# Attention, FFN and mixture of experts on one core: row maxima by way of DRAM, three-pass up products, one table set at the start

## The reference, cut to what matters

```python
x = x + xattn0(layernorm(x), ctx)        # 16 heads of 8, softmax over 256 keys
x = x + ffn0(layernorm(x))               # butterfly up, gelu, butterfly down, 512 hidden
x = x + xattn1(layernorm(x), ctx)        # 16 heads of 8
x = x + moe(layernorm(x))                # 16 experts of 64, top 4, and a shared one

scores = einsum('bhqd,bhkd->bhqk', q, k) / sqrt(8)
attn   = softmax(scores, axis=-1)
out    = einsum('bhqk,bhkd->bhqd', attn, v)
...
h = gelu(butterfly(x @ W_exp + b_exp, up_weights) + up_bias)
```

## Time and profile before

| what | us |
|---|---|
| median of 3 runs | 209.72 (208.79 to 210.5) |
| the profiled execution | 209.94 |
| its span in the trace | 207.8 |

### The profile page before, as it was taken

How to read it: one execution, slowest core, us unless ns; L and a number is a source line. 1 busy time by engine, 2 the same in 40 slices (tenths; PEclk the granted TensorE clock), 3 DMA queues, 4 the chain that set the end, 5 groups by cost and what they waited for, 6 DMA issues and landing times.

```text
span 207.8 us, 4287 instructions
## 1 busy us (share of the span) xinstructions
PE 197.7 (95%) x1727; PEld 110.7 (53%) x1727; DVE 154.2 (74%) x243; ACT 146.7 (71%) x262; POOL 55.6 (27%) x72
## 2 busy tenths in 40 slices
PE   7798899999999999997999999999999999999993
PEld 4464367564574543443344566554566745766640
DVE  0399989899998764259975989999775664795482
ACT  2865873989886999972795998987999936613230
POOL 7948940039046000059000000040000252300400
PEclk9999999999999999999999999999999999999999
DMA  6950000000004400000000000000000352003641
GB/s 177 323 224 3 0 0 5 2 3 0 3 0 131 197 3 0 0 5 0 0 0 3 0 5 0 3 0 3 0 5 6 122 205 80 0 6 136 179 142 50
DMA packets 5795, 10.50 MB, mean 51 GB/s; under 512 B 1120, under 2 KB 2576, under 8 KB 5648
## 3 DMA queue, kind: packets, MB, share of 16 engines
q1 hardware_dynamic: 4208, 6.16, 9.3%
q0 software_dynamic: 848, 3.53, 4.5%
q10 hardware_dynamic: 720, 0.53, 0.9%
HBM read 9.64 MB, written 0.59 MB: 49 GB/s over the span
## 4 chain that ended last, share of the span: by engine, by line
PE 81%; DVE 7%; ACT 4%; DMA 2%; issue 2%; SPq 1%; POOL 1%
PE PS L363 60%; PE OB L363 21%; DVE T L1003 3%; DMA spread<-comb_out 2%; SPq L658 1%; DVE attn L1033 1%; DMA comb_out<-comb_t 1%; DVE k_lo L940 1%; DVE xn L991 1%; ACT K L830 1%; POOL hid_t L777 1%; ACT sq L853 1%; ACT sq L856 1%; ACT sq L840 0%; DVE x L1047 0%
## 5 line engine op out<-in xcount | busy, mean ns | idle before, releaser
L1003 DVE TENSOR_REDUCE T<-PS 128x4 f32<-128x1024 f32 x64 | 76.6, 1220 | 4.8 <-PE PS L363 4.2
L864 ACT ACTIVATE P<-PS 128x512 f32<-128x512 f32 x128 | 68.1, 603 | 14.0 <-PE PS L363 13.3
L363 PE MATMUL OB<-P,V 128*32 128x256 f32 x512 | 33.4, 384 | 0.1
L363 PE MATMUL PS<-K,Q 32*128 32x256 f32 x256 | 28.2, 323 | 0.5 <-ACT sq L856 0.3
L363 PEld LDWEIGHTS PS<-K,Q 32*128 32x128 f32 x256 | 17.6, 183 | 17.0 <-ACT P L864 6.9
L363 PE MATMUL PS<-Q,K 32*128 32x256 f32 x256 | 25.6, 320 | 0.3
L363 PEld LDWEIGHTS PS<-Q,K 32*128 32x128 f32 x256 | 16.4, 183 | 11.5 <-ACT P L864 5.1
L777 POOL TENSOR_TENSOR hid_t<-spread,prod_t 128x512 f32<-128x512 f32 x7 | 9.3, 1325 | 46.6 <-DMA spread<-comb_out 37.3
L917 ACT ACTIVATE gate_t<-PS 128x512 f32<-128x512 f32 (+1 forms) x18 | 10.3, 596 | 16.1 <-DVE prod_t L1112 12.0
L363 PEld LDWEIGHTS OB<-P,V 128*32 128x32 f32 x512 | 14.3, 109 | 10.6 <-ACT P L864 0.9
L765 POOL TENSOR_TENSOR attn<-o_raw,sums 128x512 f32<-128x512 f32 x4 | 5.1, 1282 | 44.9 <-ACT sums L883 44.8
(11 more groups left out here) (125 smaller groups left out, 324.8 us busy)
## 6 DMA issues: line engine op xcount, KB each, us to landing
spread<-comb_out SPq DMA_DIRECT2D x32, 128.0 KB, 3.0
w_gu<-gu POOLq DMA_DIRECT2D x1, 1024.0 KB, 5.5
w<-w2p POOLq DMA_DIRECT2D x1, 512.0 KB, 5.8
outT<-x SPq DMA_DIRECT2D x2, 256.0 KB, 2.9
e_up<-eup POOLq DMA_DIRECT2D x1, 508.0 KB, 6.1
e_dn<-edn POOLq DMA_DIRECT2D x1, 508.0 KB, 6.4
w_exp<-wexp POOLq DMA_DIRECT2D x1, 258.0 KB, 6.2
x<-xT SPq DMA_DIRECT2D x2, 128.0 KB, 3.0
```

Of the source, the lines that this page charges most:

```text
L363: return nc.tensor.matmul(out, lhsT, rhs, start=start, stop=stop)
L864: finish(nc.scalar.activation(P[:, (JOINT * U + j) % (JOINT * PUNITS), :, :].rearrange("p k q -> p (k q)"), PS[:, FILLED["sc", U, j // 2][ ...
L1003: finish(nc.vector.tensor_reduce(dst, two("max", U, i).rearrange("p j (t s) -> p j t s", t=2), AX.X, ALU.max, negate=True), "red", U, i)
```

## The change

- `turn` and `shift` are gone. `red.U.i` writes into T[:, U, ...] (a place of its own for each unit). A new table for SP holds `st.U` and `ld.U`. `st.U` stores T's 128 x 8 numbers to DRAM so that each of the four heads has a row of 256 there: 1024 single numbers of 4 bytes. `ld.U` waits for that store and reads the four rows of 1 KB into row g, 32 + g, 64 + g and 96 + g of Q. `sc.U` waits for the load's semaphore. RING = 8 semaphores each serve stores and loads.
- `up` multiplies in three passes (high by high, high by low, low by high) in f32r instead of one f32 product. For it `uhi` (ACT) and `ulo` (DVE) split the normed rows, and `fwr.3` writes a high and a low part of the matrix.
- ACT loads the table set for exp and log ahead of its first computation.
- `moeadd` is two additions of half a chunk; SP stores the first half, ACT the second.
- The tables of all engines are written anew: 38 fills for 31, and steps move between engines (`xcopy`: 7 on DVE for 4, `hid`: 9 on POOL for 7).

```diff
 BANKS = 7
-TURNS = 2
 PUNITS = 3
+RING = 8
...
-sc.23.0:16 pv.21 turn.13:2 max.27.0:34 sc.23.1:05 pv.22 max.27.1:12 sc.24.0:06 pv.23 sc.24.1:35 max.28.0:12
...
+sc.23.0:23 qsel.1.1.3:4 pv.21 max.26.0:01 sc.23.1:26 max.26.1:45 pv.22 max.27.0:23 pv.23 sc.24.0:06 sc.24.1:14
...
+SP_ORDER = """
+st.0 ld.0 st.1 st.2 ld.2 ld.1 st.3 st.4 ld.3 st.5 ld.4 st.6 ld.6 ld.5 st.7 ld.7 st.9 st.8 st.10 ld.8 ld.10 ld.9
+st.11 st.12 ld.12 ld.11 st.13 st.14 ld.13 st.15 ld.14 ld.15 st.16 st.17 ld.16 st.19 st.20 st.18 ld.17 ld.18
+ld.19 ld.20 st.21 ld.21 st.22 ld.22 st.23 ld.23 st.24 ld.24 st.25 st.26 ld.25 ld.26 st.27 ld.27 st.28 st.29
+ld.28 ld.29 st.30 st.31 ld.30 ld.31
...
-        T = sb("T", [D, TURNS, 2, D])
+        T = sb("T", [D, UNITS, JOINT, 2], f32r)
...
-        w_up = sb("w_up", [D, BLK, D])
+        w_up_hi, w_up_lo = (sb(n, [D, BLK, D], f32r) for n in ("w_up_hi", "w_up_lo"))
...
+        turn_out = nc.dram_tensor("turn_out", (UNITS, JOINT, 2, D), f32, kind="Internal").ap()
...
-            def turn(t):
-
-                take()
-                for U in reversed(TURN_UNITS[t]):
-                    for i in (1, 0):
-                        after(pe, "red", U, i)
-                if fresh(pe, eye_in, 16):
-                    pe.wait_ge(eye_in, 16)
-                for qt in range(2):
-                    for j in range(JOINT):
-                        rows = slice(32 * j, 32 * j + 32)
-                        last = mm(bank("turn", t)[rows, qt * D:(qt + 1) * D], T[:, t % TURNS, qt, rows], EYE)
-                give(last, "turn", t)
...
-                after(pe, "shift", turned_with(U))
+                turned_waited(pe, U)
...
+            def three(to, w_high, w_low, high, low, start=True, stop=True):
+
+                mm(to, w_high, high, start=start, stop=False)
+                mm(to, w_high, low, start=False, stop=False)
+                return mm(to, w_low, high, start=False, stop=stop)
...
             def up(c, k):
                 take()
-                after(pe, "normed", norm(1, c))
+                after(pe, "ulo", c)
                 after(pe, "fwr", 3)
-                give(mm(bank("up", c, k), w_up[:, k, :], xn[:, chunk(c)]), "up", c, k)
+                give(three(bank("up", c, k), w_up_hi[:, k, :], w_up_lo[:, k, :], n_hi[:, :], n_lo[:, :]), "up", c, k)
...
+            def stored_waited(U):
+                if fresh(sp, turned_out[U % RING], 16 * (U // RING + 1)):
+                    sp.wait_ge(turned_out[U % RING], 16 * (U // RING + 1))
+
+            def store_maxima(U):
+                for i in (1, 0):
+                    after(sp, "red", U, i)
+                if U >= RING:
+                    stored_waited(U - RING)
+                sp.dma_start(turn_out[U].rearrange("j t q -> q j t"), T[:, U, :, :].bitcast(f32),
+                             allow_slow_non_contiguous=True).then_inc(turned_out[U % RING], 16)
+
+            def load_maxima(U):
+                l, b, g = unit(U)
+                stored_waited(U)
+                if U >= RING:
+                    turned_waited(sp, U - RING)
+                sp.dma_start(Q[g:D:32, g, queries(b)].bitcast(f32).rearrange("j (t q) -> j t q", t=2),
+                             turn_out[U]).then_inc(turned_in[U % RING], 16)
+
+            steps = {"st": store_maxima, "ld": load_maxima}
+            for name, *at in SP_STEPS:
+                steps[name](*at)
...
-                after(sp, "moeadd", c)
-                sp.dma_start(outT[:, chunk(c)], x[:, chunk(c)]).then_inc(stored, 16)
+                sp.wait_ge(half_added, c + 1)
+                half = slice(c * CH, c * CH + CH // 2)
+                sp.dma_start(outT[:, half], x[:, half]).then_inc(stored, 16)
             sp.wait_ge(stored, 16 * NCH)
+            sp.wait_ge(stored_too, 16 * NCH)
...
-            nc.gpsimd.memset(T[:, :, :, :].bitcast(u32), 0).then_inc(t_zero, 1)
...
             act.dma_start(w_v[:, :], wv).then_inc(wv_in, 16)
+            tables(EXP_LN)
...
+            def high_rows(c):
+
+                after(act, "normed", norm(1, c))
+                for v in range(NCH):
+                    filled(act, "vproj", v)
+                for p in range(len(SPANS[1])):
+                    filled(act, "kproj", 1, p)
+                if c:
+                    for k in range(BLK):
+                        filled(act, "up", c - 1, k)
+                finish(nc.scalar.activation(n_hi[:, :], xn[:, chunk(c)], ACT.Copy), "uhi", c)
...
+                act.dma_start(outT[:, half], x[:, half]).then_inc(stored_too, 16)
...
-                t = turned_with(U)
                 filled(dve, "max", U, i)
-                if fresh(dve, t_zero, 1):
-                    dve.wait_ge(t_zero, 1)
-                if t >= TURNS:
-                    filled(dve, "turn", t - TURNS)
-                dst = T[:, t % TURNS, :, :].rearrange("p t (j r) -> p j t r", r=32)[:, 2 * i:2 * i + 2, :, g]
-                finish(nc.vector.tensor_reduce(dst, two("max", U, i).rearrange("p j (t s) -> p j t s", t=2), AX.X,
+                finish(nc.vector.tensor_reduce(T[:, U, 2 * i:2 * i + 2, :], two("max", U, i).rearrange("p j (t s) -> p j t s", t=2), AX.X,
                                                ALU.max, negate=True), "red", U, i)
-
-            def shift(t):
-
-                l, b, g = unit(TURN_UNITS[t][0])
-                n = len(TURN_UNITS[t])
-                dst = Q[:, g:g + n, queries(b)]
-                filled(dve, "turn", t)
-                finish(nc.vector.tensor_tensor(dst, bank("turn", t)[:, 0:SEQ].unsqueeze(1).broadcast_to([D, n, SEQ]),
-                                               dst.bitcast(f32), ALU.add), "shift", t)
...
-                finish(nc.vector.tensor_copy(dst, src), "fwr", step)
+                if step == 3:
+                    link(nc.vector.tensor_copy(dst, src))
+                    finish(nc.vector.tensor_tensor(w_up_lo[:, :, :], src, dst.bitcast(f32), ALU.subtract), "fwr", step)
...
+            def low_rows(c):
+                after(dve, "uhi", c)
+                finish(nc.vector.tensor_tensor(n_lo[:, :], xn[:, chunk(c)], n_hi[:, :].bitcast(f32), ALU.subtract),
+                       "ulo", c)
...
-                finish(nc.vector.tensor_tensor(x[:, chunk(c)], OB[:, :], x[:, chunk(c)], ALU.add), "moeadd", c)
+                half = slice(c * CH, c * CH + CH // 2)
+                nc.vector.tensor_tensor(x[:, half], OB[:, 0:CH // 2], x[:, half], ALU.add).then_inc(half_added, 1)
+                half = slice(c * CH + CH // 2, (c + 1) * CH)
+                finish(nc.vector.tensor_tensor(x[:, half], OB[:, CH // 2:CH], x[:, half], ALU.add), "moeadd", c)
```

229 lines of the change are left out of this document (118 added, 111 removed).

## The result

| kernel | median, us | runs | against the kernel before |
|---|---|---|---|
| before, same chip | 209.89 | 4 | |
| changed | 336.88 (335.14 to 339.09) | 4 | 1.608, interval 1.600 to 1.617 |

The change makes the kernel 61% slower, by 127 us. Forecast were 202.9 us and a range of 199 to 210. The mechanism is that of rival 2 (the store lands late and SP becomes the bound), at a size beyond the upper end that I had given it.

What follows compares the result with a forecast made beforehand. PE was taken as the bound, busy 197.7 of 207.8 us, with DVE and ACT close behind in places. Terms -9.2 + 0.5 - 0.3 + 0.5 + 1.2 + 0.5 = -6.8; 209.94 - 6.8 - 0.2 = 202.9 us, range 199 to 210.

Steps and rivals of the forecast that it cites:

- rival 2: SP becomes the bound as stores land late: 215 us for a 6.5 us store, 218.6 for 7.0; chance 0.14.
- The step that failed: Pricing each unit's store of 1024 single numbers from neighbouring packet rows: 2.7 us taken, upper end 7.0.
- Seven rounds of L + 0.5: Layer 1, red.21.1 to red.31.1: SP's seven store-wait-load rounds, L being the store's time; keeps pace up to 4.0 us.
- the 5.4 us of slack: Between max.21.1 and sc.21.0: 12.5 us of other work, less 1.9 for the reduction and 5.2 for the trip.
- The load: Each unit's load of four 1 KB rows behind its store: between 1.6 and 3.0 us, 2.0 taken.
- Turns, up products and fills on PE: On PE, seventeen turns -9.4, three-pass up products -1.8, seven more fills +2.0: -9.2 us in all.
- DVE keeps the steady stretch: In 115 to 150 us DVE keeps its 32.8 us, so the stretch falls by 1.6 only: +1.2 us.
- Rival 1: DVE and ACT are the bound and PE only looks full, so gains there are lost: 206.5 us; chance 0.2.
- Up products -1.8, split +0.5: Three-pass up products save PE 1.8 us; uhi and ulo in the norm, up, gelu chain may show 0.5 at chunk 1.
- Table load 0: At the start, one early table load saves 1.25 us but the new order gives it back: 0, between -1.3 and +1.0.
- Last store -0.3: At the end, storing the first half before the second addition saves 0.3 us, between 0 and 0.6.
- Trips +0.5: Store-and-load trips of 5.2 us are mostly hidden by other work; 0.5 us added for tight places such as start and end.

Runs made afterwards that it cites:

- e7: Changed kernel storing and loading only the maxima of each unit's first 128 queries, 512 single numbers in place of 1024; 341.36 us.
- e13: Changed kernel storing maxima twice: 32 B pieces, which the load reads, and 1024 single numbers 8 B apart; the load waits for both; 299.77 us.
- e9: Changed kernel with maxima stored in 256 pieces of 16 B and read back by four loads per unit, one per head; 264.5 us, ratio 1.254.
- e2: Changed kernel with each store as 128 pieces of 32 B in place of 1024 of 4 B, maxima read back permuted; 207.19 us, ratio 0.987.
- e8b: Changed kernel storing maxima twice: 32 B pieces, which the load reads, and 1024 single numbers 64 B apart; the load waits for both; 233.52 us.
- e8: Changed kernel storing maxima twice: 32 B pieces, which the load reads, and 1024 single numbers 512 B apart; the load waits for both; 217.6 us.
- e5: Changed kernel with only SP's order changed, stores of later units ahead of a unit's load; 379.87 us.
- e1: Changed kernel without its 32 stores and 32 loads; PE waits for the reductions and the maxima are not subtracted; 204.93 us, ratio 0.975.
- e6: The kernel before with only the three-pass up products and their split of tokens and weights; 216.76 us, ratio 1.019.
- e3: Changed kernel storing 32 B pieces by query, with the load reading 1024 single numbers out of DRAM; 243.42 us, ratio 1.158.
- e12: Changed kernel with VectorE turning maxima in 32x32 blocks before the store, one turn and one store for each two units; 222.96 us, ratio 1.047.
- e10: Changed kernel with VectorE turning each unit's maxima in 32x32 blocks, so 128 B pieces go out and back; 210.9 us, ratio 1.000.
- e4: The kernel before, its order kept, with three-pass up products, one table load at the start and halved last store; 212.39 us, ratio 1.010.

## Why the prediction was wrong

**The step that failed** is "64 x 17 ns more gives 2.7 us, 64 x 42 ns gives 4.3, and twice that for a write that also reads 7.0, the upper end". The packets are even cheaper: 0.47 of 16 engines' 1 us, over the 1040 packets of that stretch, is 7 ns each. But a landing is not the sum of packets: the 6.3 us of silence come behind them. What the runs put in its place:

| store of a unit | pieces | separate writes in each 64 B | in each 512 B | landing, us |
|---|---|---|---|---|
| changed kernel | 1024 of 4 B, side by side | 16 | 128 | 10.4 |
| e7 | 512 of 4 B, side by side | 16 | 128 | 9.7 |
| e13 | 1024 of 4 B, 8 B apart | 8 | 64 | 6.6 |
| e9 | 256 of 16 B, side by side | 4 | 32 | 2.7 |
| e2 | 128 of 32 B, side by side | 2 | 16 | 1.4 |
| e8b | 1024 of 4 B, 64 B apart | 1 | 8 | 3.8 |
| e8 | 1024 of 4 B, 512 B apart | 1 | 1 | 3.1 |

What is shown: single numbers land later the closer they lie, at the same count, and half as many at the same closeness land about as late. What is not shown is a law. If the writes within 64 B cost one another, it is 0.44 us for each further one, (10.4 - 3.8) / 15, which gives 6.9 for e13 against 6.6 measured, and nothing for the difference of e8b and e8. If it is those within 512 B, it is 0.057 us for each, (10.4 - 3.1) / 127, which gives 6.7 for e13 and 3.5 for e8b against 6.6 and 3.8. Both estimates fit; both mix the distance with the order of the partitions, and neither holds for larger pieces (e9 and e2 land sooner than e8b). Whether the DMA engine or the memory holds the writes up, no run tells.

The Trainium skill's DMA: Bandwidth & Descriptors, section Specifications, has an engine read, modify and write below 512 B. That rule puts e2's, e8's and the changed kernel's pieces on the same side of its line, and they land in 1.4, 3.1 and 10.4 us: a small write can be cheap, and many small writes close together are not. Its rule for authors (section Rules for kernel authors), against a strided last dimension, holds here. My use of its Bandwidth section against it, 2.3 us for the store as an estimate, was the same mistake: a price for packets taken as a price for a landing.

**Rival 2's round was sound, and its count of rounds was not.** Seven rounds of L + 0.5 give 76.3 us with L = 10.4. From the issue of st.21 (190.06 us) to that of st.30 (264.14) the seven rounds took 74.1 us. The stretch of ten units took 92.3, because st.21 could go out only 15.3 us after its reduction had ended (174.75): SP stood at the load of an earlier unit, behind three stores issued within 3.3 us, and the last of them landed late.

```profile
170.69 17.69 DMA turn_out<-T
...
264.14 3.30 SPq L657 DMA_DIRECT2D turn_out<-T  x2
```

The remaining 2.9 us lie between the issue of st.30 and the end of red.31.1. The other place with three stores close together looks alike: of the three issued from 75.69 to 77.38 us SP waited for the last until 91.70. So stores on their way together may hold one another up, as theory W1 of e5 has it; no run tests it by itself.

For the whole kernel the formula was far too low. It counts the seven rounds of those ten units, takes off the 5.4 us of slack, and gives a loss of 39.5 us at L = 10.4, so 242 us, where 336.88 were measured. SP's table has twenty rounds for all 32 units, and 20 x 10.9 = 218 of the 261 us between the first store's issue (15.58) and the last load's (276.6). Layer 0's stores on the chain took 8.27 to 11.59 us too, and the prediction had worked out the round for layer 1 alone.

I gave this rival 0.14, because I ended its price at "twice the packets'"; that doubling was worked out from no row of such a store, and with none in the trace this cost had no upper end.

No term held the clock either. It is 0.64 in 183 to 267 us, and PE's own busy time is 228.2 us against e1's 190.5 with the same 1462 instructions. In those seven rounds SP's waits set the pace and the slower PE costs nothing; what it costs elsewhere was not separated.

The load was the second term sized too low: I took 2.0 us, between 1.6 and 3.0. It took 1.90 to 4.43 behind a landed store, and 8 to 10 with another store on its way.

**The other terms**, read from e1 and e2, where the trip costs nothing:

- Turns, up products and fills on PE, -9.2 in all: PE's busy time fell by 7.2 us to 190.5, against "about 188". Two us short.
- DVE keeps the steady stretch: forecast 31.4 us from red.21.1 to red.31.1, measured in e1 34.4 (110.65 to 145.09), longer than the 33.0 before. Between these two reductions DVE is busy 32.66 us, against 30.89 before, so its work there grew by 1.8 us where I had it unchanged. PE's fell only from 32.82 to 32.32. Rival 1 was right that this stretch gains nothing, but its sign, DVE or ACT over 97%, is not there: DVE is at 95% and PE at 94%. The gain came before it: red.21.1 ends at 110.65 instead of 116.3 us.
- Up products -1.8, split +0.5: not measured apart. In e2 the passes stand 0.24 us apart without a wait, as the 1.8 assumes. From attention's output product to the down products e1 and e2 take 14.16 us and the kernel before 13.05, with other work in between. In e6, where the split is not covered, the same way takes 3.6 us more than before.
- Table load 0: not told apart from nothing. The first reduction is at 13.3 us in e1 and 13.38 before, and between 13.2 and 15.9 over all kernels with the new start.
- Last store -0.3: from the end of the additions to the end of the span 2.3 us in e1 (199.4 to 201.7), 2.5 before (205.3 to 207.8). Right to within 0.1 (0.2 gained).
- Trips +0.5: in e2, with a landing of 1.4 us, PE waits 0.4 us. Right for a store like that one.

Together the order without a slow store is worth 204.9 us (e1) to 207.2 (e2), against the forecast of 202.9 and rival 1's 206.5: e1 lies between the two, e2 above both, and the difference did not matter beside the landing.

## What to carry to other kernels

Price a small DMA by its landing and not by its packets, and look in the trace for how long the engines are silent before it lands. 1024 numbers scattered one by one into DRAM, next to each other, landed in 10.4 us here, and in 1.4 us as 128 pieces of 32 B. Writing larger pieces or spacing them out cures the landing, but is no gain by itself: of the kernels that do the whole computation by way of DRAM (e3, e5, e9 to e12) none was shown to be faster than the one before, and e10, which turns in SBUF first, only equals it. And when the decisive operation is in no row of the trace, measure it alone before the order is built round it: my upper end from neighbouring rows was 7.0 us, and 10.4 were measured. Price a wait for every unit that has it, not only for the stretch that was looked at.

## What was not expected of the hardware

- 1024 writes of 4 B: 10.4 us side by side, 3.1 us at 512 B apart; 512 of them side by side 9.7 us. 1024 reads of 4 B: 4.75 us, on about four of 16 engines when they fill four rows.
- A load of four rows issued 0.4 us behind such a store came in after 8 to 10 us (e5), instead of 1.90 to 4.43.
- In e6 1.34 us of waiting in PE's stretch of norms and FFN was followed by 6 us at a granted clock of 0.50, and the two together cost 3.6 us. A wait of 1.32 us in the kernel before was not followed by any fall.
- Loads of weights that ran beside the single-number stores landed later too: w_gu in 10.8 us (e5 10.6, e7 11.4, e13 7.6), against 5.5 before and 5.0 to 5.2 in e2, e4, e6, e8, e8b and e10.
